# Second graph layer: 26 candidates a table row, penalties inside the same products, 11 and 12 TensorE columns a table, one-hot tiles by two ScalarE passes

## The reference

```
x = layernorm(x + layer1(x, src, dst, ...))
e = leaky_relu((x @ a[:32])[src] + (x @ a[32:])[dst])        # one number per edge
ex = exp(e - segment_max(e, dst)[dst])
out = segment_sum(x[src] * (ex / segment_sum(ex, dst)[dst]), dst)
x = layernorm(x + out)
```

## Time and profile before

| what | value |
|---|---|
| median of 3 runs | 4710.45 us (4707.23 to 4713.73) |
| span of the profiled execution | 4706.6 us |
| PE busy in it | 3382.1 us, 72% |
| DVE busy | 3188.3 us, 68% |
| ACT busy | 1353.5 us, 29% |
| POOL busy | 3428.1 us, 73% |
| second layer's loop | about 2873 to 4548 us |

### The profile page before, as it was taken

How to read it: one execution, slowest core, us unless ns; L and a number is a source line. 1 busy time by engine, 2 the same in 40 slices (tenths; PEclk the granted TensorE clock), 3 DMA queues, 4 the chain that set the end, 5 groups by cost and what they waited for, 6 DMA issues and landing times. The chain is left out here.

```text
span 4706.6 us, 64422 instructions
## 1 busy us (share of the span) xinstructions
PE 3382.1 (72%) x20039; PEld 1884.8 (40%) x20039; DVE 3188.3 (68%) x5351; ACT 1353.5 (29%) x2662; POOL 3428.1 (73%) x3518
## 2 busy tenths in 40 slices
PE   0005888888888888888887004999999999999950
PEld 0001333333323333233322003777777777777740
DVE  4525999999999999999997312555555555555532
ACT  3003555555555555555553000000101001010100
POOL 5776777777777777777773776777777777777766
PEclk9999999999999999999999557999999999999975
DMA  9512222222222222222221001222222222222211
GB/s 329 153 36 43 46 54 45 45 52 45 45 54 45 46 52 45 50 49 45 52 45 25 12 17 32 45 51 50 50 50 47 42 49 50 50 50 50 42 25 26
DMA packets 266563, 251.69 MB, mean 53 GB/s; under 512 B 182208, under 2 KB 236936, under 8 KB 263777
## 3 DMA queue, kind: packets, MB, share of 16 engines
q1 hardware_dynamic: 157028, 174.83, 13.8%
q0 software_dynamic: 109024, 72.30, 10.9%
q10 hardware_dynamic: 462, 4.00, 0.3%
HBM read 160.54 MB, written 90.34 MB: 53 GB/s over the span
## 5 line engine op out<-in xcount | busy, mean ns | idle before, releaser
L607 POOL DMA_INDIRECT edge<-xp_d,idx x1440 | 1415.5, 983 | 537.8 <-issue 391.4
L1194 POOL DMA_INDIRECT gxb<-tab_d,idxb x1200 | 1288.4, 1074 | 376.4 <-issue 320.3
L859 DVE TENSOR_TENSOR prod<-G_ps,hid 128x1000 f32<-128x1000 f32 x1200 | 1399.2, 1193 | 124.4 <-PE G_ps L742 110.1
L742 PE MATMUL G_ps<-FT,wst 32*128 32x500 f32 x4800 | 896.6, 633 | 369.1 <-DVE prod L859 366.7
L1229 PE MATMUL G_ps<-tb,hot 125*126 125x500 f32 (+1 forms) x3200 | 680.1, 366 | 337.3 <-DVE hotk L1251 300.6
L1229 PEld LDWEIGHTS G_ps<-tb,hot 125*126 125x126 f32 x3200 | 550.3, 193 | 454.0 <-issue 350.7
L771 PE MATMUL R_ps<-prod,red 128*32 128x500 f32 x4800 | 589.0, 593 | 0.0
L742 PEld LDWEIGHTS G_ps<-FT,wst 32*128 32x128 f32 x4800 | 246.3, 183 | 804.9 <-DVE prod L859 751.7
L663 ACT ACTIVATE hid<-T_ps 128x500 f32<-128x500 f32 x400 | 233.1, 583 | 721.1 <-PE T_ps L762 684.4
L762 PE MATMUL T_ps<-FT,wst 32*128 32x500 f32 x800 | 432.3, 620 | 3.1 <-ACT FT L659 3.1
L1257 DVE TENSOR_REDUCE gxb<-G_ps 125x20 f32<-125x500 f32 (+1 forms) x400 | 211.8, 576 | 315.0 <-PE G_ps L1232 315.0
(11 more groups left out here) (242 smaller groups left out, 4373.6 us busy)
## 6 DMA issues: line engine op xcount, KB each, us to landing
xd_d<-zeros SPq DMA_DIRECT2D x16, 1562.5 KB, 29.1
y_d<-zrb SPq DMA_DIRECT2D x40, 595.0 KB
edge<-xp_d,idx POOLq DMA_INDIRECT x1440
xv<-xd_d SPq DMA_DIRECT2D x40, 560.0 KB
y_d<-zr SPq DMA_DIRECT2D x40, 560.0 KB
edge<-sel_d SPq DMA_DIRECT2D x40, 546.9 KB
gxb<-tab_d,idxb POOLq DMA_INDIRECT x1200
em<-in_edge_attr SPq DMA_DIRECT2D x40, 175.0 KB
```

The source lines that it names most:

```text
L607: nc.gpsimd.indirect_dma_start(out=edge_c[:, i, 8:8 + DIM], out_offset=None, in_=xp_d, in_offset=bass.IndirectOffsetOnAxis(col, 0)).then_i ...
L742: return Tn.matmul(G_ps[pair][:, a * 512:a * 512 + GW], wst[rows, r * 128:(r + 1) * 128], FT[k][rows, :], start=True, stop=True)
L859: V.tensor_tensor(prod[b][i][:, :].rearrange("p (a e) -> p a e", a=2), gv, hid[k][:, :].rearrange("p (a e) -> p a e", a=1).broadcast_to([1 ...
L1194: nc.gpsimd.indirect_dma_start(out=gx[h][:, c * T1:(c + 1) * T1], out_offset=None, in_=tab_d, in_offset=bass.IndirectOffsetOnAxis(idx[h][: ...
```

## The change

Nothing changes in the first layer. In the second:

- A table row holds KL = 26 nodes, so 481 rows hold all 12,500 (padded to 12,506), and 4 groups of 128 partitions hold 512 rows. The 31 rows left over take the penalties: rows 0 to 30 of the last group (26 of them used) are what `far` was. A column is then 2 x 4 pairs of products, 442 and 416 columns wide, and no pair with `far`.
- `tb` is built from `tab_d`: SP reads it back in four DMAs (128, 128, 128 and 97 rows) once it is written, then ScalarE and VectorE convert it.
- TensorE takes 11 columns of an h = 0 chunk and 12 of an h = 1 chunk, POOL 29 and 28 gathers. POOL waits for `d_col` only once a chunk.
- The one-hot tiles are made by ScalarE: |node - row| (Abs), then Relu(1 - that), for each of 4 groups, 128 partitions and 1375 or 1500 columns. In ScalarE's queue this stands between the exponentials and the copies into `zr`.
- In the first stage the row numbers and the numbers inside a row are worked out for 23 columns a turn instead of 20, by 26 instead of by 100 and 25, and written to `sel_d` in 115 rows instead of 100.
- `load_nodes` gives the row number to 128 partitions, and for the last group a tile `nodek` whose rows 0 to 30 hold the number inside the row and rows 31 to 127 the row number.

```diff
-    XC = 10
-    KL = 25
+    XCS = (11, 12)
+    CGS = tuple(C - w for w in XCS)
+    KL = 26
+    HI = -(-N // KL)
+    R3 = 31
-    FU = 20
-    GS = KL * (DIM + 1) + 1
+    FU = 17
+    GS = KL * (DIM + 1)
...
     @block.sync   # between the layers
+                    for i in range(NG4):
+                        lo = R3 if i == NG4 - 1 else 0
+                        sp.dma_start(tbl[lo:128, i * GS:(i + 1) * GS],
+                                     tab_d.rearrange("(r k) f -> r (k f)", k=KL)[i * 128:min(HI, i * 128 + 128 - lo), :]).then_inc(S("c_tbl"), 16)
...
     @block.sync   # second layer
-                    def load_nodes(ch, h):
+                    def load_nodes(ch, h, t):
                         if not isinstance(ch, int):
-                            sp.wait_ge(S("d_hot"), ch * 5 - 5)
+                            sp.wait_ge(S("d_hot"), ch * NG4 - NG4)
                             sp.sem_inc(S("go"), 1)
-                        for a, t in ((0, nodes[h]), (1, nodek[h])):
-                            rows = sel_d[a]....broadcast_to([t.shape[0], XP])
-                            if a == 0:
-                                by_rows(sp, t, rows, S(f"d_nd{h}"))
-                            else:
-                                sp.dma_start(t, rows).then_inc(S(f"d_nd{h}"), 16)
+                        hi, k = [sel_d[a]....rearrange("(a f) -> a f", a=1) for a in range(2)]
+                        sp.dma_start(nodes[h], hi.broadcast_to([128, XPS[h]])).then_inc(S(f"d_nd{h}"), 16)
+                        sp.dma_start(nodek[h][0:R3], k.broadcast_to([R3, XPS[h]])).then_inc(S(f"d_nd{h}"), 16)
+                        sp.dma_start(nodek[h][R3:128], hi.broadcast_to([128 - R3, XPS[h]])).then_inc(S(f"d_nd{h}"), 16)
...
     @block.gpsimd
-                                pool.wait_ge(S("d_col"), (t * 2 + h) * XC - 1)
+                                pool.wait_ge(S("d_col"), cols_before(t * 2 + h, h, t) - 1)
                                 pool.sem_inc(S("go"), 1)
-                            for c in range(CG):
-                                if c % 3 == 0 and c > 3:
-                                    pool.wait_ge(S("d_col"), (t * 2 + h) * XC + c // 3 - 1)
-                                    pool.sem_inc(S("go"), 1)
+                            for c in range(CGS[h]):
...
     @block.scalar
-                    def chunk(h, t):
+                    def one_hot(ch, h, t):
+                        act.wait_ge(S(f"d_nd{h}"), t * 48 + 48)
+                        act.sem_inc(S("go"), 1)
+                        if not isinstance(ch, int):
+                            act.wait_ge(S("d_col"), cols_before(ch - 1, 1 - h, t - 1 + h))
+                            act.sem_inc(S("go"), 1)
+
+                        def distance(g):
+                            if g >= 2 or not isinstance(ch, int) or ch > 0:
+                                act.wait_ge(S("d_hot"), ch * NG4 + g - 1)
+                            nc.scalar.activation(ab[g % 2][:, 0:XPS[h]], nodek[h] if g == NG4 - 1 else nodes[h], ACT.Abs, bias=niot[:, g:g + 1]).then_inc(S("d_ab"), 1)
+
+                        def equal(g):
+                            act.wait_ge(S("d_ab"), ch * NG4 + g + 1)
+                            nc.scalar.activation(hot[h][:, g * XPS[h]:(g + 1) * XPS[h]], ab[g % 2][:, 0:XPS[h]], ACT.Relu, bias=ones[:, 0:1], scale=-1.0).then_inc(S("d_hot"), 1)
+
+                        distance(0)
+                        for g in range(NG4):
+                            if g + 1 < NG4:
+                                distance(g + 1)
+                            equal(g)
+
+                    def chunk(h, t, more=True):
                         act.wait_ge(S("d_pre"), t * 2 + h + 1)
                         nc.scalar.activation(wx[...], ex[:, 0:C], ACT.Exp).then_inc(S("d_exp"), 1)
                         nc.scalar.activation(ex[:, C:2 * C], ex[:, C:2 * C], ACT.Exp).then_inc(S("d_exp"), 1)
+                        if more:
+                            one_hot(t * 2 + h + 2, h, t + 1)
                         act.wait_ge(S(f"d_st{h}"), t * 32)
...
     @block.tensor
                         for l in range(2):
                             for g in range(NG4):
                                 for (f0, f1, w), ps in zip(FUS, slot):
-                                    nc.tensor.matmul(...)
-                        for (f0, f1, w), ps in zip(FUS, slot):
-                            last = nc.tensor.matmul(ps[0:PE2, 0:w], hotk[h][:, j * P:j * P + PE2], far[:, 0:w], start=False, stop=True)
+                                    last = nc.tensor.matmul(...)
...
     @block.vector
-                            one_hot(t * 2 + h + 2, h, t + 1)
-                            for j in range(XC):
-                                pick(t * 2 + h + 1, 1 - h, j)
+                            for j in range(XCS[1 - h]):
+                                pick(t * 2 + h + 1, 1 - h, j, t + h)
```

More of the change, by code:

```diff
@@ L56, in gnn_resnorm_kernel @@
     C121 = 1.5 ** 0.5
-    XC = 10
-    CG = C - XC
+    XCS = (11, 12)
+    XCP = sum(XCS)
+    CGS = tuple(C - w for w in XCS)
     NG4 = 4
-    KL = 25
-    XP = XC * P
-    FU = 20
-    GS = KL * (DIM + 1) + 1
+    KL = 26
+    HI = -(-N // KL)
+    R3 = 31
+    assert 128 * (NG4 - 1) + 128 - R3 >= HI and R3 >= KL
+    XPS = tuple(w * P for w in XCS)
+    XPM = max(XPS)
+    FU = 17
+    GS = KL * (DIM + 1)
     PE2 = P + 1
@@ L992, in gnn_resnorm_kernel @@
         both = ExitStack()
-        tb = [both.enter_context(nc.sbuf_tensor(f"tb{l}", [P, NG4 * GS], f32r)) for l in range(2)]
-        far = both.enter_context(nc.sbuf_tensor("far", [KL, FU * KL], f32r))
-        assert NG4 * KL == NP and KP == KL and NPIECE == NG4
+        tb = [both.enter_context(nc.sbuf_tensor(f"tb{l}", [128, NG4 * GS], f32r)) for l in range(2)]
         with ExitStack() as st:
@@ L1119, in gnn_resnorm_kernel @@
             NS = len(SLOTS)
-            assert 2 * XC % NS == 0
+            LATE = XCP % NS
+            assert LATE == NS - 1 and XCS[0] >= LATE
+            ab = [sbt(f"ab_{g}", [128, XPM]) for g in range(2)]
+            niot = sbt("niot", [128, NG4])
             sdr = two("sdr", C)
@@ L1212, in chunk, with column @@
                         nc.scalar.activation(zo[:, :, 0:T1], Zv[h][:, 1:], ACT.Copy).then_inc(S(f"d_zr{h}"), 1)
-                    with act.Fori(0, PAIRS) as t:
+                    act.wait_ge(S("d_init"), 1)
+                    for h in range(2):
+                        one_hot(h, h, 0)
+                    with act.Fori(0, PAIRS - 1) as t:
                         for h in range(2):
                             chunk(h, t)
+                    for h in range(2):
+                        chunk(h, PAIRS - 1, more=False)
                 @block.tensor
                 def _(pe):
-                    def column(ch, h, j):
-                        q = ch * XC + j
+                    def column(ch, h, j, t):
+                        q = cols_before(ch, h, t) + j
+                        i = h * XCS[0] + j
                         if j == 0:
-                            pe.wait_ge(S("d_hot"), ch * 5 + 5)
-                        pe.wait_ge(S("d_red"), q * 2 + 2)
-                        slot = SLOTS[(h * XC + j) % NS]
+                            pe.wait_ge(S("d_hot"), ch * NG4 + NG4)
+                        pe.wait_ge(S("d_red"), q * 2 + (4 if i < LATE else 2))
+                        slot = SLOTS[i % NS]
                         for l in range(2):
@@ L1236, in _ @@
                         for h in range(2):
-                            for j in range(XC):
-                                column(t * 2 + h, h, j)
+                            for j in range(XCS[h]):
+                                column(t * 2 + h, h, j, t)
                 @block.vector
```

139 lines of the change are left out of this document (69 added, 70 removed).

## The result

The changed kernel takes 5175.8 us (median of 4 runs, 5173.91 to 5179.8) against 4709.55 for the kernel before beside it: a ratio of 1.099, with a 95% interval of 1.0975 to 1.1006. The change is 466 us slower. The forecast was 5230, in a range of 5030 to 5430. The profiled span is 5175.3 us, 50.7 less than the sum of the prediction.

A forecast was written before the change was run, and what follows sets the result against it. POOL's gathers bound the kernel before (41.4 us a chunk); after the change, one-engine node-row transfers in a ring would. 37 turns of 54.8 us put chunk 39's read at 5059, 519 us later: span 5226, runs about 5230, range 5030 to 5430.

The forecast's parts named there:

- a ring with ScalarE and SP: Second layer's loop: node rows of c+3 are requested only after those of c+2 landed and were used; likeliest case, 0.81.
- The turn: One chunk of the second layer's loop: 54.8 us, against 41.5 before; bounds 49.6 and 61.5 us.
- eight passes: ScalarE's one-hot tile: eight passes of 1.35 or 1.45 us, 11.2 less overlap, so 10.6 us (10.0 to 11.5).
- two copies into `zr`: ScalarE after the one-hot tile: 0.2 + 2.8 us, 3.0 us a chunk.
- SP to the next node DMA: SP's queue, from the end of ScalarE's copy to the next node DMA: 5.0 us with the wake-up.
- issue to ScalarE's start: Node rows: 1.0 us to first bytes, 31.3 for bytes on one engine, 2.9 sharing with gathers, 1.0 landing.
- The start: Second layer's first chunks: node rows of chunk 0 land at 2911, chunk 1 at 2946, chunk 2 at 2979 us.
- the rival at 5530 us: TensorE stays at the low clock, a column taking 5.3 us and 11.5 of them 61 us: about 5530 us, chance 0.03.
- Table loads: ScalarE's Abs and Relu beside Exp: possibly 0 to 2.6 us a chunk, taken as 0.
- POOL at 38.5 us a chunk: POOL's 28.5 gathers a chunk in the second layer: 38.5 us, 2.9 less than before if every wait stayed.
- the rival "about 4600": Node rows spread over the engines land in some 6 us and POOL decides: about 4600 us, chance 0.12.
- The stage between the layers: Reading the table back, 13 us on one engine, and conversions: costed at nothing under POOL's scatters; 30 us once without cover.

The follow-up runs named there:

- experiment 1: Changed kernel with penalty rows at 30 instead of 31, so node rows go as 128, 30 and 98: 4603.97 us, ratio 0.977 to the kernel before.
- 3 to 5: Changed kernel with one node-row transfer cut in two: 31 as 16 + 15, 97 as 37 + 60, 97 as 1 + 96: 4925.8, 4692.7, 4605.3 us.
- experiment 2: Changed kernel, 31 and 97 rows kept, with ScalarE's copies into `zr` ahead of the one-hot tile: 4624.25 us, ratio 0.9815 to the kernel before.
- the kernel before with 113 rows: Kernel before the change with its 125 node rows loaded as 113 + 12 instead of 112 + 13: 4732.24 us, ratio 1.0045.
- VectorE's tiles: Kernel with 30 and 98 rows, its one-hot tiles built by four VectorE passes again: 4624.6 us, ratio 0.983 to the kernel before.
- 9 and 10 columns: Kernel with 30 and 98 rows, TensorE taking 9 and 10 columns instead of 11 and 12: 4686.45 us, ratio 0.9946 to the kernel before.
- 37 + 60: Changed kernel with its transfer of 97 node rows cut into 37 and 60: 4692.7 us, ratio 0.9975 to the kernel before.

## Why the prediction was right, step by step

- **The mechanism was right and is shown.** The transfers of 31 and 97 rows run on one engine each (experiments 1 and 3 to 5, and the 31.5 us in which SP's queue holds a sixteenth of the engines), they lie in a ring with ScalarE and SP (experiment 2), and the ring, not POOL, sets the period. The prediction cites the divisor rule of the Trainium skill, DMA: Bandwidth & Descriptors, "Why a DMA increments its semaphore by 16 and not by 1"; the runs agree, 5175.8 us with 31 and 97 rows against 4604.0 with 30 and 98 above all, and they do not show which engines are taken.
- **The turn:** 54.8 forecast, 53.54 measured. Its terms, from the turn shown above and the next:

| term | forecast | measured |
|---|---|---|
| eight passes | 10.6 | 10.95 (1375 columns), 11.8 (1500): 11.4 |
| two copies into `zr` | 3.0 | 2.73 |
| SP to the next node DMA | 5.0 | 4.97 and 5.41: 5.2 |
| issue to ScalarE's start | 1.0 + 31.3 + 2.9 + 1.0 = 36.2 | 35.9 and 32.9: 34.4 |
| sum | 54.8 | 53.7 |

- **What makes up the 50.7 us between sum and span.** 37 turns that were 1.25 us too long in the forecast make 46, a third tile that is done 7 us earlier (2982.0, forecast 2989) makes 7, and an end that is 2.7 us longer takes that back. Some of the closeness is luck: inside the turn, passes that were priced 0.8 us too short stand against a transfer priced 1.8 us too long.
- **Where the 1.8 us of the last term are.** The cuts price 136 rows at 136 x 0.223 = 30.3 us, sharing with the gathers included; I had 31.3 + 2.9 = 34.2. What is left beside the bytes is 34.4 - 30.3 = 4.1 us, and I had 2.0 for issue and landing. So the bytes were priced too dear and the two ends too cheap. Sharing costs little: SP's queue moves 0.26 MB in 2930 to 2940 us, 26 GB/s with no gather in flight, and 25 GB/s beside the gathers, while I had taken 25 and added 2.9 us for them.
- **The passes** were taken from 1600 columns in 1536 ns, by a slope that gave 1.35 and 1.45 us. They take 1.43 and 1.53, eight of them 11.9 us and not 11.2, so 1500 columns take as long here as 1600 in that row. The slope was the mistake; the overlap of neighbours, 0.5 us, is close to the 0.6 that I took. Line 446 is a square root without a bias tile, and these passes have one; whether that is the difference was not tried.
- **The start:** first tile started at 2909.54 (forecast 2911), the second at 2941.97 (2946), the third at 2970.94 (2979). Chunk 39's picks end 41.4 us after its tile (41.6 forecast), but its read comes 2.9 us after them: POOL waited 19 us for indices and issued the last gather at 5006.09.
- **TensorE:** the timeline of one chunk in the changed kernel, and the windows of chunk 39 (length, busy time of PE, PEld, DVE, ACT and POOL, granted clock, DMA share, GB/s):

```profile
3408.16 8.58 PE L1274 MATMUL G_ps<-tb,hot 128*126 128x442 f32 x32 [11.56 <-ACT hot L1232]
3416.58 3.32 PE L1274 MATMUL T_ps<-tb,hot 128*126 128x442 f32 x16
3419.74 0.36 PE L1274 MATMUL R_ps<-tb,hot 128*126 128x442 f32 x1
```

```profile
4960.00:4965.00 5.00, 0.57 (x2) 0.54 (x3) 0.00 (x0) 5.00 (x5) 0.00 (x0) 0.50 0.00 0
4965.00:4970.00 5.00, 5.00 (x17) 4.66 (x16) 2.79 (x2) 2.35 (x4) 0.00 (x0) 0.58 0.41 130
4970.00:4975.00 5.00, 5.00 (x27) 4.76 (x26) 4.87 (x8) 1.41 (x1) 2.15 (x3) 1.00 0.12 22
```

A column is 3419.74 - 3416.58 = 3.16 us. The forecast took 3.2, between 3.14 (with the `far` pair's extra time gone) and 3.31 (without). The first two take 8.42 where two more would be 6.3: the 2 us that the prediction added. In chunk 39 TensorE starts at 4964.43 after 18 us of idleness; the granted clock is 0.50 (1.2 GHz) at first, 0.58 in the mean of the next 5 us and 1.00 (2.4 GHz) from 4970 on, so the rival at 5530 us did not come.
- **Table loads:** none added, as forecast, 11 in 22 chunks. These rows agree with the statement of the Trainium skill (ScalarE: Activation LUTs, "Table sets: the hidden batching unit") that abs and relu stand in every set of tables.
- **POOL at 38.5 us a chunk** was the second term behind the ring: 38.53 in experiment 1, and the rival "about 4600" came out at 4604. Of the saving, one-hot tiles off VectorE are 0.86 us a chunk (1.0 forecast) and a gather and a half less the rest.
- **The stage between the layers** was costed at nothing, and costs nothing. Its lines in the changed kernel, SP's loads, the two engines' conversions and POOL's last scatter that ends the stage, answer to the earlier trace rows:

```profile
2748.41 1.63 SPq L1113 DMA_DIRECT2D tbl<-tab_d  x4
2767.51 6.65 ACT L1099 ACTIVATE tb<-tbl 128x858 fp32r<-128x858 f32 x4 [32.76 <-DMA tbl<-tab_d]
2769.28 6.88 DVE L1071 TENSOR_TENSOR tb<-tbl,tb 128x858 fp32r<-128x858 f32 x4 [28.17 <-ACT tb L1099]
```

```profile
2862.21 1.24 POOL L1049 DMA_INDIRECT hsd<-sdt_d,head_i  x1 [0.30 <-issue]
```

The conversions end at 2776.2, 86 us before the scatter.

What the experiments got wrong as a group was not the loop but its start: of the four expectations that missed by more than a microsecond, three (the kernel before with 113 rows, VectorE's tiles, 9 and 10 columns) had the period right to 0.2 us and left out 11 to 31 us before the first chunk; the fourth (37 + 60) also let the ring bind from the first turn.

## What to carry to other kernels

Look at the row count of each transfer that is waited for: 31 and 97, two prime numbers in an edit that was about other engines, cost 572 us here, and a change of one row took them back. A slow transfer alone need not cost anything; follow its request back through the queues and ask whether it is issued only after the last one has been used, and if it is, break the ring or shorten the transfer. When two kernels differ by a period, price their starts apart: a period binds only from where its slack is used up.

## What was not expected of the hardware

- SP itself is held while transfers with only one engine are in flight. At the start of the second layer, where node rows of three chunks are asked for in a row, pairs of issues that take 0.8 us otherwise take up to 14.9, and single ones of 0.26 us up to 7.6. SP's queue in the changed kernel:

```profile
2876.54 0.35 SPq L1166 DMA_DIRECT2D edge<-sel_d  x1
...
2877.76 14.87 SPq L78 DMA_DIRECT2D idxb<-in_src  x2
...
2899.78 6.54 SPq L1168 DMA_DIRECT2D edge<-sel_d  x1
```

The same is seen in the kernel before with 113 rows, up to 22.5 us for one pair of issues. Small loads that stand behind it on SP are late by as much. That a full queue of the one engine is the reason is a guess and was not tried.

- At the start of the second layer, 30 and 98 rows (and the 128) are used 7.0 us after their issue (2877.11, first pass at 2884.13), 31 and 97 rows 33.0 us after theirs (2876.54, 2909.54).
- The tile order has a side effect that the prediction did not name: the exponents of the next chunk stand behind the one-hot tile on ScalarE, and VectorE waited for them by up to 12.9 us in the changed kernel (224 us in 1200). POOL waited up to 19.4 us for indices, which SP loads only behind the store. Neither costs anything here, since both engines had the time; in experiment 1 the first falls to 8.6 us and the second is gone.
